# Row-addressed stores from GpSimd in the experts' phase of a two-layer transformer kernel

## The chip, the cores and the metric

The kernel runs on one core of a Trainium2 chip. The metric is the device time of one execution in microseconds (us); before the change its median over 3 runs was 2280.21 us (2277.04 to 2282.47). Engines are named as in the profile: PE (matrix multiply, with PEld for its weight loads), DVE (vector), ACT (activation), POOL (GpSimd) and SP (the engine that here only issues transfers).

## The reference, cut to what matters

The input x has 128 batches of 64 tokens of width 128, that is 8192 rows of 128 float32 numbers. Four blocks follow one another, each added to x:

```
x = x + L0_xattn(layernorm(x), ctx)          # cross attention, 16 heads
x = x + L0_ffn(layernorm(x))                 # 8 experts, each takes its 8 best tokens of a batch
x = x + L1_xattn(layernorm(x), ctx)          # self attention, cross attention, relu block
x = x + L1_ffn(layernorm(x))                 # 16 routed experts (4 per token) + 2 shared ones
return x
```

The last block is the one that the change touches. For each token it computes

```
combine = (one_hot(topk_idx, 16) * tw[..., None]).sum(1)      # 4 experts of 16, weights sum to 2.5
h = einsum('td,edf->etf', x, gate_w);  u = einsum('td,edf->etf', x, up_w)
y = einsum('etf,efd->etd', silu(h) * u, down_w)
out = x + einsum('etd,te->td', y, combine) + (silu(x @ sh_gate) * (x @ sh_up)) @ sh_down
```

The result is stored to HBM as 8192 rows of 512 bytes.

## The kernel before, in words

The program is a chain of phases (setup, attention 0, choice, attention 1, attention 2, relu, experts), each with its own instruction streams for the five engines and a barrier at its end. The phase in question is `experts_phase`. It works in 16 groups of 4 tiles of 128 tokens (`NG` = 16, `TILES` = 4, `TOK` = 512). x stays in SBUF as `x_res`. In a group, `step` runs over 18 experts k (2 shared, 16 routed): PE makes the gate and up products of expert k for all 512 tokens in three partial products each (L1152 to L1154), ACT applies silu (L1102), DVE multiplies (L1313, tile `moe_act`), and PE makes the down product of expert k-2 (L1138; L1147 for the two shared ones). DVE adds it into `acc` (L1325 for the first, L1331 for most others). For four of the experts ACT weighs the product into `part` instead (L1095), and POOL sums these (L1029).

Work of the next group is threaded into the same loop: at k = 0 DVE takes its statistics, POOL makes 1/std with a power (L1044), at k = 2 DVE applies the norm (`norm_apply`, L1201, four tiles, written to `xn`), at k = 3 PE transposes these (`make_xT`, L1117), ACT copies the transposes (L1064, L1065), POOL makes the low part of x from them (`low_rows`, L1006), and in later slots DVE and POOL rank the experts (L1011 and L1013 are POOL's share).

Each engine's stream is in program order; the loops run two groups a turn (`pipelined`). POOL's order within a step is: power for group g+1; `total(g-1)`, which adds `part` to `acc` (L1034) once DVE has finished the last expert of group g-1, at k = 2; `low_rows(g+1)`; then the sums and the ranking. `total` gives `totals`, on which SP waits; SP stores `acc[:, s]` with one transfer of 256 KB (L990). `acc` has two buffers; the first write to one (L1325) waits until the store of two groups earlier has landed (`stored`).

Of the kernel before, what the change touches and what calls it, by code (L numbers as in the profile page):

```python
# [9 lines left out]
I32 = mybir.dt.int32  # L10
# [25 lines left out]
for _n, _w in [("a0", ATTN_W), ("a1", ATTN_W), ("a2", ATTN_W), ("ident", P), ("headmask", 4),  # L36
               ("g1", D), ("b1", D), ("g2", D), ("b2", D), ("g3", D), ("b3", D), ("ff2b", D),
               ("negmask", P), ("kiota", 64), ("resetmask", 256), ("trig", P), ("wr", 32),
               ("ff1", 4 * D), ("ff1b", 4), ("ff2", 4 * D), ("router", 16), ("rbias", 64),
               ("lowmask", 256), ("glowmask", 16), ("ident4", 2 * S)]:  # L40
    COLS[_n] = (_at, _w)
    _at += _w
PACK = _at
# [635 lines left out]
def nth(g, n=1, k=0):  # L679

    return g * n + (k + 1)
# [193 lines left out]
def experts_phase(nc, ps, C, x_res, gate, up, down, w_loaded, out):  # L875

    with ExitStack() as ctx:
# [81 lines left out]
        acc_done = sem("acc_done")  # L959
        part_added = sem("part_added")  # L960
        totals = sem("totals")
        stored = [sem(f"stored{s}_") for s in (0, 1)]

        def one_by_one(t):
# [14 lines left out]

        @block.sync  # L980
        def _(sp):

            for s in (0, 1):
                sp.sem_inc(stored[s], 1)
            with sp.Fori(0, NG // 2) as i:
                for s in (0, 1):
                    g = i * 2 + s

                    sp.wait_ge(totals, nth(g))
                    sp.dma_start(out[bass.ds(g * TOK, TOK), :].rearrange("(t p) d -> p t d", p=P), acc[:, s]  # L990
                                 ).then_inc(stored[s], 16)
            for s in (0, 1):
                sp.wait_ge(stored[s], 16 * (NG // 2) + 1)

        @block.gpsimd
        def _(pool):
            def prep(g, s):
                pool.wait_ge(var_eps, nth(g))
                nc.gpsimd.tensor_tensor(rstd[:, :], veps[:, :], C["mhalf"][:, 0:TILES], ALU.pow).then_inc(rstd_done, 1)
                low_rows(g, s)  # L1000

            def low_rows(g, s):

                pool.wait_ge(x_high, nth(g))
                pool.wait_ge(xT_copied, nth(g))
                nc.gpsimd.tensor_tensor(x_lo[:, s], xnT[:, s], x_hi[:, s], ALU.subtract).then_inc(x_split, 1)  # L1006

            def rank_experts(g):

                pool.wait_ge(routing, before(g, 21))  # L1010
                nc.gpsimd.tensor_tensor(by_tile(eeq), by_tile(eeq), C["lowmask"].unsqueeze(1).broadcast_to((P, TILES, E * E)), ALU.mult).then_inc(routing, 1)  # L1011
                pool.wait_ge(routing, before(g, 22))
                nc.gpsimd.tensor_tensor(by_tile(egt), by_tile(egt), by_tile(eeq), ALU.add).then_inc(routing, 1)  # L1013

            def split_weights():

                for i in range(K // CH):
                    part = slice(i * CH, (i + 1) * CH)
                    pool.wait_ge(w_high, i + 1)
                    nc.gpsimd.tensor_tensor(gate_lo[:, part], gate[:, part], gate_hi[:, part], ALU.subtract)  # L1020
                    nc.gpsimd.tensor_tensor(up_lo[:, part], up[:, part], up_hi[:, part], ALU.subtract
                                            ).then_inc(w_split, 1)

            def add_part(g, j):

                if j > 1:
                    pool.wait_ge(part_added, nth(g, len(OTHERS) - 1, j - 2))
                pool.wait_ge(acc_done, nth(g, K - 1, OTHERS[j] - SH + 1))
                nc.gpsimd.tensor_tensor(part[:, 0], part[:, 0], part[:, j], ALU.add).then_inc(part_added, 1)  # L1029

            def total(g, s):
                pool.wait_ge(part_added, (g + 1) * (len(OTHERS) - 1))
                pool.wait_ge(acc_done, (g + 1) * (K - 1))
                nc.gpsimd.tensor_tensor(acc[:, s], acc[:, s], part[:, 0], ALU.add).then_inc(totals, 1)  # L1034

            def first_prep(g, s):
                prep(g, s)
                split_weights()
                rank_experts(g)

            def step(g, s, first, more):
                if more:
                    pool.wait_ge(var_eps, nth(g + 1))
                    nc.gpsimd.tensor_tensor(rstd[:, :], veps[:, :], C["mhalf"][:, 0:TILES], ALU.pow  # L1044
                                            ).then_inc(rstd_done, 1)
                if not first:
                    total(g - 1, 1 - s)
                if more:
                    low_rows(g + 1, 1 - s)
                add_part(g, 1)  # L1050
                if more:
                    rank_experts(g + 1)
                add_part(g, 2)
                add_part(g, 3)
                if not more:
                    total(g, s)

            pipelined(pool, NG, first_prep, step)

        @block.scalar  # L1060
        def _(act):
# [121 lines left out]
        def _(dve):  # L1183
# [131 lines left out]
            def accumulate(g, s, k):  # L1315

                if k < SH - 1 or k in OTHERS:
                    return
                n = k - SH + 1
                dve.wait_ge(y_ready, nth(g, K - 1, n))  # L1320
                y = YB[k % 2].rearrange("p (t d) -> p t d", d=D)
                if n == 0:

                    dve.wait_ge(stored[s], g * 8 + (1 - 8 * s))
                    V.tensor_tensor(acc[:, s], y, tiles_of(x_res, g), ALU.add).then_inc(acc_done, 1)  # L1325
                    return
                dve.wait_ge(acc_done, nth(g, K - 1, n - 1))
                if n == 1:
                    dve.wait_ge(routing, nth(g, NR, NR - 1))
                for t in range(TILES):  # L1330
                    last = V.scalar_tensor_tensor(acc[:, s, t], y[:, t], comb[:, s, t, k - SH:k - SH + 1], acc[:, s, t],  # L1331
                                                  ALU.mult, ALU.add)
                last.then_inc(acc_done, 1)
# [583 lines left out]
def setup_phase(nc, ps, C, pack_in, q_mask, pack, work):  # L1917

    with ExitStack() as ctx:
# [27 lines left out]
        @block.vector  # L1947
        def _(dve):
            nc.vector.memset(C["mhalf"][:, :], -0.5)
            nc.vector.memset(C["half"][:, :], 0.5)  # L1950
            nc.vector.memset(C["oneb"][:, :], 1.0 / 32)
            nc.vector.memset(work["ones"][:, :], 1.0).then_inc(consts_set, 1)
            dve.wait_ge(pack_loaded, 16)
            for a in range(3):
                bias = COLS[f"a{a}"][0] + 5 * D
                nc.vector.tensor_scalar(C["bkm"][:, a, :], C["headmask"], pack[:, bias + 1:bias + 2], None, ALU.mult
                                        ).then_inc(consts_set, 1)
            bias = COLS["a0"][0] + 5 * D
            nc.vector.tensor_scalar(C["bqs"][:, :], pack[:, bias:bias + 1], SCALE, None, ALU.mult).then_inc(consts_set, 1)
            nc.vector.tensor_copy(C["identb"].rearrange("p f k -> p (f k)"), C["ident4"]).then_inc(consts_set, 1)  # L1960
            dve.wait_ge(qmask_loaded, 64)
            nc.vector.tensor_scalar(C["qmask"], work["qmi"][:, :, :], 0.0, NEG, ALU.is_equal, ALU.mult
                                    ).then_inc(qbias_done, 1)
            dve.wait_ge(qbias_done, 1)
            nc.vector.tensor_reduce(work["any"][:, 0:2], C["qmask"], AX.X, ALU.max).then_inc(qany_done, 1)
            dve.wait_ge(qany_done, 1)
            nc.vector.tensor_scalar(work["any"][:, 2:4], work["any"][:, 0:2], 0.0, SCALE, ALU.is_equal, ALU.mult
                                    ).then_inc(qany_done, 1)
            dve.wait_ge(qany_done, 2)
            for f in (0, 1):  # L1970
                nc.vector.tensor_scalar(work["diag"][:, f, :], C["ident4"][:, S * f:S * f + S],
                                        work["any"][:, 2 + f:3 + f], None, ALU.mult).then_inc(qscale_diag, 1)
            dve.wait_ge(qscale_ready, 1)
            nc.vector.tensor_copy(C["qscale"][:, :], ps[:, 1, 0:64]).then_inc(qscale_copied, 1)


def build(nc, x_in, ctx_in, q_mask, key_mask, pack_in, wqkv_in, woe_in, gate_in, up_in, down_in, out):
    with ExitStack() as ctx:
# [7 lines left out]
        for n, (at, w) in COLS.items():  # L1986
# [6 lines left out]
        C["half"] = sb("half", [P, 8])  # L1993
        C["qmask"] = sb("qmask", [P, 2, S], BF16)[:, :, :]
        C["qscale"] = sb("qscale", [P, S])
        work = {"qmi": sb("qmi", [P, 2, S], I32), "ones": sb("ones", [P, P]), "any": sb("qany", [P, 4]),
                "diag": sb("qdiag", [P, 2, S])}
        setup_phase(nc, ps, C, pack_in, q_mask, pack, work)
# [87 lines left out]
```

## Time and profile before

| | us |
|---|---|
| median of 3 runs | 2280.21 |
| lowest, highest | 2277.04, 2282.47 |
| the profiled execution's own time | 2276.67 |
| its span, first to last instruction | 2274.7 |
| PE busy in the span | 2021.8 (89%) |
| DVE busy | 1738.6 (76%) |
| ACT busy | 1015.3 (45%) |
| POOL busy | 511.8 (23%) |

The experts' phase begins at about 1540 us of the span and lasts to its end. In the row of the profile's page that cuts the span in 40 slices PE shows 8 or 9 tenths in every slice of it but the first, and POOL 2 or 3. Line numbers (L1034) are those of the kernel before. A row of the timeline gives the start, the duration, the engine, the line, what is written and read with its size, and the number of instructions merged in the row; in brackets stands how long the engine was idle before it, and what ended that. "SPq" is the stream of transfers that SP issues.

### The profile page before, as it was taken

To read this page: it belongs to the slowest core of one execution; us is meant where nothing else is said; L and a number is where in the kernel's file an instruction comes from. 1 tells how busy PE (TensorE), PEld (TensorE's weight loads), DVE (VectorE), ACT (ScalarE), POOL (GpSimd) and SP (SyncE) were. 2 spreads that over 40 slices of the span, in tenths; PEclk is the share of its full clock that TensorE was granted. 3 is DMA by queue.
4 is the path that set the end of the run, shared out by engine and by line. 5 is a ranking of instruction groups with operands and counts; after the bars stand their busy time and mean duration, and the time that the engine had idled before them with its cause. 6 is when DMAs were issued, how large, how long until landed. Compare 5 with 4: busy or idle time off the path is not lost. (4 is left out here: it accounts for less than half of the span.)

```text
span 2274.7 us, 52942 instructions
## 1 busy us (share of the span) xinstructions
PE 2021.8 (89%) x19268; PEld 1557.3 (68%) x19268; DVE 1738.6 (76%) x4586; ACT 1015.3 (45%) x1956; POOL 511.8 (23%) x504
## 2 busy tenths in 40 slices
PE   5999995777777999997999997994999999999998
PEld 3666664566664666664677675764888888888887
DVE  4767766677755888887799995665888888888886
ACT  3455452445542444443455553543444444443443
POOL 0101100000001222322122222663222232232221
PEclk9999998899996999998999998996999999999999
DMA  3000000000000000000000001000000000000000
GB/s 121 20 28 28 18 18 1 1 1 0 0 1 1 1 0 0 0 0 19 30 28 28 28 18 63 1 0 0 6 6 10 5 5 10 5 5 9 6 5 10
DMA packets 27248, 30.41 MB, mean 13 GB/s; under 512 B 1936, under 2 KB 20624, under 8 KB 26896
## 3 DMA queue, kind: packets, MB, share of 16 engines
q1 hardware_dynamic: 27152, 29.28, 4.1%
q8 instruction: 42, 0.69, 0.1%
q14 instruction: 54, 0.44, 0.1%
HBM read 25.08 MB, written 4.19 MB: 13 GB/s over the span
## 5 line engine op out<-in xcount | busy, mean ns | idle before, releaser
L320 ACT ACTIVATE ex<-ps 128x512 f32<-128x512 f32 x384 | 228.7, 596 | 335.7 <-PE ps L580 334.5
L1102 ACT ACTIVATE moe_sg<-ps 128x512 f32<-128x512 f32 x288 | 172.6, 599 | 365.0 <-PE ps L1154 364.8
L414 DVE TENSOR_REDUCE mx<-ps 128x8 f32<-128x512 f32 x384 | 262.5, 684 | 62.0 <-PE ps L562 61.2
L580 PEld LDWEIGHTS ps<-pack,sh 128*128 128x128 f32 x1536 | 173.9, 144 | 185.0 <-DVE sh L416 113.3
L580 PE MATMUL ps<-pack,sh 128*128 128x128 f32 x1536 | 253.7, 289 | 44.4 <-DVE sh L416 43.1
L1138 PEld LDWEIGHTS ps<-down,moe_act 128*128 128x128 f32 x2048 | 266.1, 191 | 33.9 <-DVE moe_acc L1331 13.0
L1138 PE MATMUL ps<-down,moe_act 128*128 128x128 f32 x2048 | 271.0, 275 | 7.3 <-DVE moe_acc L1331 7.3
L416 DVE TENSOR_TENSOR sh<-ps,mx 128x512 f32<-128x512 f32 x384 | 265.6, 692 | 13.2
L596 PEld LDWEIGHTS ps<-vblk,ex 128*64 128x64 f32 x6144 | 215.1, 140 | 66.8 <-issue 66.2
L596 PE MATMUL ps<-vblk,ex 128*64 128x32 f32 x6144 | 258.1, 228 | 0.3
L1313 DVE TENSOR_TENSOR moe_act<-ps,moe_sg 128x512 f32<-128x512 f32 x288 | 197.7, 686 | 69.2 <-PE ps L1154 55.2
L1331 DVE SCALAR_TENSOR_TENSOR moe_acc<-ps,moe_comb,moe_acc 128x128 f32<-128x128 f32 x768 | 215.6, 343 | 22.3 <-issue 15.5
L562 PE MATMUL ps<-kblk,qd 32*64 32x256 f32 x3072 | 210.8, 392 | 0.0
L287 ACT ACTIVATE kblk<-ps,bkm,pack 128x512 f32<-128x512 f32 x192 | 143.1, 778 | 69.7 <-PE ps L527 56.8
L1152 PE MATMUL ps<-moe_x_lo,moe_gate_hi 128*128 128x512 f32 x288 | 137.3, 477 | 26.3 <-DVE moe_act L1313 24.8
L562 PEld LDWEIGHTS ps<-kblk,qd 32*64 32x64 f32 x3072 | 108.4, 136 | 52.2 <-issue 6.7
L224 POOL TENSOR_TENSOR rstd<-veps,mhalf 128x4 f32<-128x4 f32 x32 | 32.6, 1017 | 388.4 <-DVE veps L376 388.4
L1029 POOL TENSOR_TENSOR moe_part<-moe_part 128x512 f32<-128x512 f32 x48 | 62.2, 1295 | 253.9 <-ACT moe_part L1095 253.9
L250 POOL TENSOR_TENSOR zg<-z,pack 128x256 f32<-128x256 f32 x64 | 40.8, 638 | 334.3 <-DVE z L459 334.3
L1154 PE MATMUL ps<-moe_x_hi,moe_gate_hi 128*128 128x512 f32 x288 | 114.3, 397 | 0.0
L1152 PE MATMUL ps<-moe_x_lo,moe_up_hi 128*128 128x512 f32 x288 | 114.2, 396 | 0.0
L1153 PE MATMUL ps<-moe_x_hi,moe_gate_lo 128*128 128x512 f32 x288 | 114.0, 396 | 0.0
(232 smaller groups left out, 3663.7 us busy)
## 6 DMA issues: line engine op xcount, KB each, us to landing
ctxT<-in_ctx SPq DMA_DIRECT2D x32, 256.0 KB, 2.8
x_res<-in_x SPq DMA_DIRECT2D x16, 256.0 KB, 2.9
kmi<-in_key_mask SPq DMA_DIRECT2D x16, 256.0 KB, 3.4
out<-moe_acc SPq DMA_DIRECT2D x16, 256.0 KB, 2.3
pack<-in_pack SPq DMA_DIRECT2D x1, 2536.5 KB, 9.2
wqkv<-in_wqkv SPq DMA_DIRECT2D x1, 1536.0 KB, 8.5
gate<-in_gate SPq DMA_DIRECT2D x6, 192.0 KB, 4.0
up<-in_up SPq DMA_DIRECT2D x6, 192.0 KB, 4.1
```

Of the source, the lines that this page charges most:

```text
L287: last = nc.scalar.activation(kblk[:, s, :, j, :], by_batch(PREP), ACT.Identity, bias=bkm[:, j:j + 1], scale=headmask[:, j:j + 1])
L320: nc.scalar.activation(ex[:, u % 2], UB[u % 4].rearrange("p (c n) -> p c n", n=P), ACT.Exp).then_inc(e_ready, 1)
L414: nc.vector.tensor_reduce(mx[:, u % 2], sc, AX.X, ALU.max).then_inc(max_done, 1)
L416: nc.vector.tensor_tensor(sh[:, u % 4].rearrange("p (h k) -> p h k", k=S), sc, mx[:, u % 2].unsqueeze(2).broadcast_to((P, HH, S)), ALU.sub ...
L562: last = nc.tensor.matmul(outs[w][64 * b:64 * b + 64, t * HQ * S:(t + 1) * HQ * S], qd[rows, s, n * S:(n + 1) * S], kblk[rows, s, n].rearr ...
L580: last = nc.tensor.transpose(UB[u % 4][:, c * P:(c + 1) * P], sh[:, u % 4, c * P:(c + 1) * P], ident)
L596: last = nc.tensor.matmul(OB[m][64 * b:64 * b + 64, col:col + 32], ex[:, u % 2, c, b * S:(b + 1) * S], vblk[:, s, 2 * (2 * m + t) + b, pai ...
L1102: nc.scalar.activation(sg[:, k % 2], GB_[k % 2], ACT.Silu).then_inc(silu_done, 1)
L1138: last = nc.tensor.matmul(YB[k % 2][:, t * D:(t + 1) * D], act_[:, k % 3, t * P:(t + 1) * P], down[:, k, :], start=True, stop=True)
L1152: nc.tensor.matmul(out, hi, y, start=True, stop=False)
L1313: V.tensor_tensor(act_[:, k % 3], UB[k % 2], sg[:, k % 2], ALU.mult).then_inc(act_ready, 1)
L1331: last = V.scalar_tensor_tensor(acc[:, s, t], y[:, t], comb[:, s, t, k - SH:k - SH + 1], acc[:, s, t], ALU.mult, ALU.add)
```

## The change

- `out` is no longer written by SP. After each `total`, POOL copies four columns of row numbers into a tile `rowid`, waits for that copy and for its own sum, and then issues four indirect transfers, one for each tile of 128 tokens: partition p of `acc[:, s, t]` goes to the row of `out` whose number stands in `rowid[p, s, t]`. Each counts 16 into `stored[s]`.
- The row numbers are laid into the packed constants on the host (64 more columns, 0 to 8191 column by column) and turned to integers in setup by one more DVE instruction.
- SP's loop now waits for the four transfers of a buffer and gives two counts to a new semaphore `acc_free[s]`, on which DVE's first write of the buffer waits, instead of waiting on `stored[s]` itself. At the end of the phase it is POOL that waits for all transfers.

```
             for s in (0, 1):
-                sp.sem_inc(stored[s], 1)
+                sp.sem_inc(acc_free[s], 1)
             with sp.Fori(0, NG // 2) as i:
                 for s in (0, 1):
-                    g = i * 2 + s
-                    sp.wait_ge(totals, nth(g))
-                    sp.dma_start(out[bass.ds(g * TOK, TOK), :].rearrange("(t p) d -> p t d", p=P), acc[:, s]
-                                 ).then_inc(stored[s], 16)
-            for s in (0, 1):
-                sp.wait_ge(stored[s], 16 * (NG // 2) + 1)
+                    sp.wait_ge(stored[s], (i + 1) * (16 * TILES))
+                    sp.sem_inc(acc_free[s], 2)
...
                 nc.gpsimd.tensor_tensor(acc[:, s], acc[:, s], part[:, 0], ALU.add).then_inc(totals, 1)
+                nc.gpsimd.tensor_copy(rowid[:, s], C["rows"][:, bass.ds(g * TILES, TILES)]).then_inc(rows_set, 1)
+                pool.wait_ge(rows_set, nth(g))
+                pool.sem_inc(passed, 1)
+                pool.wait_ge(totals, nth(g))
+                pool.sem_inc(passed, 1)
+                for t in range(TILES):
+                    nc.gpsimd.indirect_dma_start(
+                        out, bass.IndirectOffsetOnAxis(rowid[:, s, t:t + 1], 0), acc[:, s, t], None
+                    ).then_inc(stored[s], 16)
...
             pipelined(pool, NG, first_prep, step)
+            for s in (0, 1):
+                pool.wait_ge(stored[s], 16 * TILES * (NG // 2))
...
-                    dve.wait_ge(stored[s], g * 8 + (1 - 8 * s))
+                    dve.wait_ge(acc_free[s], g + (1 - s))
                     V.tensor_tensor(acc[:, s], y, tiles_of(x_res, g), ALU.add).then_inc(acc_done, 1)
...
             nc.vector.tensor_scalar(C["bqs"][:, :], pack[:, bias:bias + 1], SCALE, None, ALU.mult).then_inc(consts_set, 1)
+            nc.vector.tensor_copy(C["rows"][:, :], C["rowid"]).then_inc(consts_set, 1)
...
+    put("rowid", np.arange(BATCH * S).reshape(-1, P).T)
```

On POOL, in the experts' loop, this stands around the sum `total` (`moe_acc<-moe_acc,moe_part`) and the low part of x (`moe_x_lo`) before the change:

```order
193 L1032 ISA
194 L1033 REGISTER_ALU
195 L1034 TENSOR_TENSOR moe_acc<-moe_acc,moe_part 128x512
196 L1006 TENSOR_TENSOR moe_x_lo<-moe_xnT,moe_x_hi 128x512
197 L1028 REGISTER_ALU
198 L1029 TENSOR_TENSOR moe_part<-moe_part 128x512
```

and this after it, at the same place (`rows` is the constant table of row numbers, `moe_rowid` the tile that the transfers read):

```order
193 L1030 ISA
194 L1031 REGISTER_ALU
195 L1032 TENSOR_TENSOR moe_acc<-moe_acc,moe_part 128x512
196 L1033 ISA
197 L1033 COPY moe_rowid<-rows 128x4
198 L1039 DMA out<-moe_acc,moe_rowid 8192x128 x4
199 L1004 TENSOR_TENSOR moe_x_lo<-moe_xnT,moe_x_hi 128x512
200 L1026 REGISTER_ALU
```

One small copy and four transfers have moved in between the sum and the low part of x. At the end of POOL's stream, in the last group, the order after the change is:

```order
238 L1027 TENSOR_TENSOR moe_part<-moe_part 128x512 x3
239 L1032 TENSOR_TENSOR moe_acc<-moe_acc,moe_part 128x512
240 L1033 COPY moe_rowid<-rows 128x4
241 L1039 DMA out<-moe_acc,moe_rowid 8192x128 x4
242 L878 UNCONDITIONAL_BRANCH
```

The last sum, which was the last of POOL's instructions in the phase, is now followed by the copy and the four transfers.

## Rows read from the trace of the kernel before

**Rows 1.** Page: busy time of each engine, and the chain that ended last, by engine.

```profile
PE 2021.8 (89%) x19268; PEld 1557.3 (68%) x19268; DVE 1738.6 (76%) x4586; ACT 1015.3 (45%) x1956; POOL 511.8 (23%) x504
...
PE 25%; DVE 4%; issue 2%; ACT 0%; DVEq 0%; POOL 0%; POOLq 0%
```

**Rows 2.** Windows, one group each: length, PE, PEld, DVE, ACT, POOL busy, clock, DMA.

```profile
1707.00:1750.00 43.00, 42.78 (x266) 37.77 (x266) 37.49 (x109) 18.77 (x39) 11.78 (x8) 1.00 0.02 6
1750.00:1795.00 45.00, 43.04 (x267) 37.64 (x266) 37.26 (x109) 18.76 (x39) 11.82 (x8) 1.00 0.02 7
```

**Rows 3.** Waits, 1560 to 2275 us: us in total, times, longest.

```profile
PE ps L1152 <- DVE moe_act L1313: 24.8, 7, 17.1
...
DVE moe_acc L1331 <- issue: 15.5, 13, 2.2
```

**Rows 4.** Timeline around the sum of one group, from 2188.3 us.

```profile
2188.56 1.28 POOL L1034 TENSOR_TENSOR moe_acc<-moe_acc,moe_part 128x512 f32<-128x512 f32 x1 [1.73 <-DVE moe_acc L1331]
...
2189.00 1.71 DVE L1201 TENSOR_SCALAR moe_xn<-x_res,moe_mv,moe_rstd 128x128 f32 x4
2189.12 1.95 PE L1147 MATMUL ps<-down,moe_act 128*128 128x128 f32 x16
...
2190.79 0.47 PEld L1117 LDWEIGHTS ps<-pack,moe_xn 128*128 128x128 f32 x4
...
2191.11 0.69 DVE L1313 TENSOR_TENSOR moe_act<-ps,moe_sg 128x512 f32<-128x512 f32 x1 [0.40 <-PE ps L1147]
...
2192.76 1.28 POOL L1006 TENSOR_TENSOR moe_x_lo<-moe_xnT,moe_x_hi 128x512 fp32r<-128x512 f32 x1 [2.91 <-ACT moe_xnT L1065]
```

**Rows 5.** Lines L1201 and L1331: duration in ns min/median/max, first and last start.

```profile
L1201 DVE TENSOR_SCALAR moe_xn<-x_res,moe_mv,moe_rstd x64: 330/336/936, 1543.5 to 2190.4; 128x128 f32 x56, 128x128 f32<-128x128 f32 x8
...
L1331 DVE SCALAR_TENSOR_TENSOR moe_acc<-ps,moe_comb,moe_acc x768: 335/343/354, 1582.4 to 2269.5; 128x128 f32<-128x128 f32 x192
```

**Rows 6.** Timeline of DVE, cut to the first and the last of that group's four.

```profile
2189.00 0.93 DVE L1201 TENSOR_SCALAR moe_xn<-x_res,moe_mv,moe_rstd 128x128 f32 x1
...
2190.11 0.59 DVE L1201 TENSOR_SCALAR moe_xn<-x_res,moe_mv,moe_rstd 128x128 f32 x2
```

**Rows 7.** A second place where DVE and POOL meet: line L1267, and the timeline.

```profile
L1267 DVE TENSOR_SCALAR moe_gout<-moe_gin x16: 164/170/1271, 1561.4 to 2208.5; 128x16 f32<-128x16 f32 x16
...
1682.69 1.30 POOL L1029 TENSOR_TENSOR moe_part<-moe_part 128x512 f32<-128x512 f32 x1 [14.44 <-ACT moe_part L1095]
1682.75 1.27 DVE L1267 TENSOR_SCALAR moe_gout<-moe_gin 128x16 f32<-128x16 f32 x1
```

**Rows 8.** POOL's instructions by size: duration in ns min/median/max.

```profile
L2080 POOL MEMSET const-float32-0.0<- x1: 98/98/98, 0.2 to 0.2; 128x1 f32 x1
...
L231 POOL COPY xn<-y_res x16: 608/609/610, 1070.2 to 1358.6; 128x512 f32 x14, 128x512 f32<-128x512 f32 x2
...
L224 POOL TENSOR_TENSOR rstd<-veps,mhalf x32: 1007/1017/1025, 20.8 to 1022.6; 128x4 f32<-128x4 f32 x32
...
L1013 POOL TENSOR_TENSOR moe_egt<-moe_egt,moe_eeq x16: 2337/2390/2397, 1566.7 to 2216.5; 128x1024 f32<-128x1024 f32 x16
```

**Rows 9.** Timeline of the end of the span.

```profile
2269.94 1.26 POOL L1034 TENSOR_TENSOR moe_acc<-moe_acc,moe_part 128x512 f32<-128x512 f32 x1 [6.81 <-DVE moe_acc L1331]
2271.37 0.37 SPq L990 DMA_DIRECT2D out<-moe_acc  x1
```

**Rows 10.** The store to `out`: issue time in ns, and us from issue to landing.

```profile
L990 SPq DMA_DIRECT2D out<-moe_acc x16: 372/372/411, 1621.4 to 2271.4; - x16
...
DMA to landing us min/median/max: 2.3/2.3/2.5
```

**Rows 11.** Timeline of setup, once the packed constants have landed.

```profile
9.99 0.49 DVE L1956 TENSOR_SCALAR bkm<-pack 128x4 f32<-128x4 f32 x3 [8.84 <-DMA pack<-in_pack]
...
10.45 0.21 DVE L1960 CAST identb<-pack 128x128 bf16<-128x128 f32 x1
```

**Rows 12.** The next instruction of POOL after L1006 in the same group.

```profile
2208.49 1.30 POOL L1029 TENSOR_TENSOR moe_part<-moe_part 128x512 f32<-128x512 f32 x1 [14.44 <-ACT moe_part L1095]
```

More of the change, by code:

```diff
@@ L39 @@
                ("ff1", 4 * D), ("ff1b", 4), ("ff2", 4 * D), ("router", 16), ("rbias", 64),
-               ("lowmask", 256), ("glowmask", 16), ("ident4", 2 * S)]:
+               ("lowmask", 256), ("glowmask", 16), ("ident4", 2 * S),
+               ("rowid", BATCH * S // P)]:
     COLS[_n] = (_at, _w)
@@ L961, in experts_phase @@
         totals = sem("totals")
+        rows_set = sem("rows_set")
+        acc_free = [sem(f"acc_free{s}_") for s in (0, 1)]
+        rowid = sb("rowid", [P, 2, TILES], I32)
         stored = [sem(f"stored{s}_") for s in (0, 1)]
@@ L1995, in build @@
         C["qscale"] = sb("qscale", [P, S])
+        C["rows"] = sb("rows", [P, NG * TILES], I32)
         work = {"qmi": sb("qmi", [P, 2, S], I32), "ones": sb("ones", [P, P]), "any": sb("qany", [P, 4]),
```

## The prediction

> **What bounds the kernel now.** The page comes first: PE is busy for 89% of the span, DVE for 76%, POOL for 23%, and the chain that ended last is mostly PE [rows 1]. Then the windows of the experts' phase, one group each: PE is busy for 42.8 of 43 us in one group and for 43.0 of 45 us in the next, at full clock [rows 2]. So PE bounds this phase, and the two odd microseconds of every second group are the question of the third view, the waits: PE waited seven times on DVE's product, 17.1 us of it once at the phase's start, so 7.7 us in the other six, and DVE itself stood up to 2.2 us for nothing but "issue", thirteen times, 15.5 us together [rows 3]. That is the turn of the loop. POOL has most of each group free. A store of `out` is on the path only once, in the last group; elsewhere it has a whole group (43 us) before its buffer is written again, against 2.3 us to land [rows 2, 10].
>
> The fourth view, the timeline around the place where the change puts its new work, matters most. POOL's sum runs from 2188.56 to 2189.84. DVE's four norm instructions run from 2189.00 to 2190.71, and PE begins to load the transposes' weights at 2190.79, 0.08 us after them, while its own earlier matmuls end at 2191.07 [rows 4]. PE therefore has next to nothing in hand there: what DVE's norm loses at this place, PE loses.
>
> DVE already loses something to POOL there. The norm instruction takes 336 ns in the median and 936 at most [rows 5]; the long one is the first of the four, 0.93 us, and it ends 0.09 us after POOL's sum does [rows 4, 6]. The same is seen elsewhere: a DVE instruction over 16 columns takes 170 ns in the median and 1271 ns where it stands beside POOL's 1.30 us sum [rows 7]. DVE's accumulations, which take one input from PSUM, are never long, 354 ns at most in 768 [rows 5]; so the norm instructions are the ones at risk.
>
> **The change part by part.**
>
> *End of the kernel.* Before, the last sum ends at 2269.94 + 1.26 = 2271.20, SP issues at 2271.37 and the data lands 2.3 us later, at 2273.7 [rows 9, 10]: 2.5 us after the sum. Now come the copy and its wait, 0.3 us together (a copy between POOL's 98 ns memset of one column and its 609 ns copy of 512 [rows 8], nearer the first, and two short waits), then four issues on POOL one behind the other, T each, and from the end of the last issue to landing what is left of the 2.3 us behind SP's 0.37 us issue, 1.9 us [rows 10]. That is 2.2 + 4T against 2.5, so 4T - 0.3 more. T has no row, since POOL issues no transfer before. Below it is bounded by SP's 0.37 us for all 512 rows [rows 10], above by POOL's longest instruction, 2.39 us over 1024 columns [rows 8]: +1.2 to +9.3 us. I take T = 1.1 us, close to the 1.02 us that POOL needs for a power over four columns [rows 8], because software that treats 128 row numbers should look like POOL's work on few columns with much to do for each. That gives +4.1 us. A transfer could also be quicker than that after its issue; 1.9 us is taken for both kinds.
>
> The Trainium skill ("DMA: Bandwidth & Descriptors", Latency and other measured facts) gives 0.6 us to the first byte for transfers issued by SP and about 1 us for those from GpSimd; by that the sum would be 0.4 us higher, an estimate. No row of before shows a GpSimd transfer.
>
> *The copy of row numbers, in 14 groups.* It starts right behind the sum, at about 2189.9, when three of DVE's four norm instructions are still to run. It is a POOL instruction that reads and writes SBUF, like the sum that held the first of them back. At 0.1 to 0.2 us, held once in each of the 14 groups that norm a next one (56 of the 64 norm instructions lie in these [rows 5]), it costs 0 to 2.8 us; I take 0.1 us each, 1.4 us.
>
> *The issues of the transfers, in the other 15 groups.* POOL works through them from about 2190.2 to 2194.6, then does the low part of x, 1.8 us later than its old start at 2192.76. Its next instruction came at 2208.49, after 14.44 us of idling [rows 4, 12], and PE needs the low part only in the next group. That delay costs nothing. Behind POOL's new wait on its own sum and copy stand only these issues.
>
> *SP's relay and DVE's wait.* DVE now waits for a count that SP passes on after the landing. The last of four landings at about 2196.5 comes some 80 us before that buffer is next written; free. SP has nothing else queued.
>
> *Setup.* One more DVE conversion of 64 columns stands in a chain where 128 columns took 0.21 us, and the constants are 1.3% longer in a load of some 9 us [rows 11]: 0.1 + 0.1 = 0.2 us.
>
> Sum: 4.1 + 1.4 + 0.2 = 5.7 us. On the profiled execution's own 2276.67 us that is 2282.4; this execution lies 3.5 us under the median of the three runs, so against 2280.21 it is 2285.9 us. Slower by 0.25%. What a measurement of this kernel can tell from no change is about 0.2%, 4.6 us.
>
> **The rivals.**
>
> *POOL's issues hold DVE's norm back as its sums do (rival 1).* The first issue starts near 2190.2, and DVE's last norm instruction near 2190.4 (the last two run 2190.11 to 2190.70 [rows 6]). If an issue holds whatever the sum held, for all its T, one norm instruction ends T late, and if DVE and POOL take turns, two of them. The bounds are 0.5 us (half an issue) and 2 x 1.2 us per group, times 14: 7 to 34 us. With one issue of 1.1 us it is 15.4 us on top of 5.7: 2301 us. For it speaks that the sum did exactly this in every group [rows 5]; against it, that building a transfer is not a pass over a tile, and that the last norm instruction may be ahead of it by the 0.2 us in question. It would also do nothing at the end of the kernel, where DVE is idle.
>
> The Trainium skill ("SBUF — State Buffer", Who interferes with whom) says that a GpSimd instruction and certain VectorE ones, tensor_scalar among them, share a port pair, and whichever is first keeps it for the whole instruction. The rows of the sum agree with that (0.93 us instead of 0.34); whether the issue of a transfer counts as such an instruction no row here shows. By that rule this rival is the case.
>
> *The turn of the loop gets cheaper (rival 2, not slower).* DVE's stream in the loop loses two rows that only wait, since its new wait folds into others. If the 2.2 us stand at the turn, which cost PE 7.7 / 6 = 1.3 us each time [rows 3], went away in all seven turns, 9.0 us would come back: 5.7 - 9.0 = -3.3, 2276.9 us. It decides only from 5.7 us, that is where at least four or five turns lose their stall. Nothing in the trace says that a stall at a branch depends on two rows more or less, so it is unlikely.
>
> *A cheap issue (rival 3).* With T near SP's 0.4 us the end costs 1.3 us, the copy hides, and setup adds 0.2: 2281.7 us, which no measurement would tell from before. For it speaks only that SP does it so; POOL has no small instruction over 0.1 us that isn't a power.
>
> **How the numbers follow.** The forecast case 0.48 (its own range 2283 to 2290: T from 0.6 to 1.8 us with the copy at 0 to 0.2 us), rival 1 0.34, rival 3 0.13, rival 2 0.05. The range of 8 in 10 leaves out the cheapest issue and rival 2 below, and the upper quarter of rival 1 above: 2281 to 2304 us. Slower by over 0.2% means above 2284.8: nearly all of rival 1 (0.33) and six tenths of the forecast case (0.30), 0.63. Faster by as much is below 2275.6: 0.04, from rival 2. The rest, 0.33, is within 0.2%.
>
> **What the profile would show.** Right: POOL's issues at the end are back to back, about 1.1 us apart, and the last one is followed by 2 us of nothing; a norm instruction of the first three kinds stays at 0.34 us, and PE's transposes start 0.1 us later behind the sum than before. Rival 1: two long norm instructions in a group instead of one, and PE idle for about 1 us before the transposes in each of 14 groups, so that a pair of groups takes 90 us or more instead of 88. Rival 2: DVE's "issue" waits fall under 10 us. Wrong altogether would be a low part of x that reaches PE late, or a first write of `acc` that waits for SP.

## The result, and the profile after

The changed kernel takes 2287.93 us (median of 18 runs) against 2281.07 us for the kernel before (18 runs, same chip): 1.0033 times as long, 95% interval 1.0022 to 1.0043, that is +5.0 to +9.8 us. It is slower, by 0.3%. The profiled execution took 2285.41 us with a span of 2283.6, which is 8.7 us more than the profiled one of before.

The page of the changed kernel, its busy times and its queues (answers to [rows 1]):

```profile
span 2283.6 us, 53027 instructions
...
PE 2023.7 (89%) x19268; PEld 1558.5 (68%) x19268; DVE 1737.5 (76%) x4587; ACT 1016.4 (45%) x1956; POOL 578.0 (25%) x584
...
q0 software_dynamic: 2048, 4.20, 0.6%
```

POOL is busy for 66 us more, which is the 64 issues and 16 copies, and a queue has appeared that carries the 4.20 MB of the output. PE and DVE do the same work as before.

The same two windows as in [rows 2], one group each (length, then busy time of PE, PEld, DVE, ACT, POOL, then clock and transfers):

```profile
1706.00:1749.00 43.00, 42.48 (x264) 37.58 (x265) 37.44 (x109) 18.46 (x39) 15.94 (x13) 1.00 0.02 6
1749.00:1794.00 45.00, 43.23 (x267) 37.62 (x265) 37.16 (x108) 19.11 (x40) 15.92 (x13) 1.00 0.02 7
```

POOL has 4 us more in each, PE nothing. From the first sum of the phase to the last it is 649.96 us before (1619.98 to 2269.94) and 649.32 after (1619.58 to 2268.90). So the groups cost nothing that can be seen. The timeline of one group shows why (answers to [rows 4]):

```profile
2187.74 1.28 POOL L1032 TENSOR_TENSOR moe_acc<-moe_acc,moe_part 128x512 f32<-128x512 f32 x1 [1.71 <-DVE moe_acc L1340]
...
2188.17 1.70 DVE L1210 TENSOR_SCALAR moe_xn<-x_res,moe_mv,moe_rstd 128x128 f32 x4
...
2188.97 0.18 POOL L1033 COPY moe_rowid<-rows 128x4 int32 x1
...
2190.07 1.08 POOL L1039 DMA_INDIRECT out<-moe_acc,moe_rowid  x1 [0.92 <-POOL moe_rowid L1033]
...
2191.45 0.96 POOL L1039 DMA_INDIRECT out<-moe_acc,moe_rowid  x1 [0.30 <-issue]
```

The copy lies inside DVE's four norm instructions and they still take 1.70 us. The first issue starts at 2190.07, 0.2 us after the last norm instruction (2188.17 + 1.70 = 2189.87), because 0.92 us pass between the copy and it. The two don't meet here. Nor do they elsewhere by the norm's durations: its four instructions keep the times that they had (minimum, median, maximum 330, 335 and 935 ns, against 330, 336 and 936 before [rows 5]; mean of the 56 in the loop 482 against 483).

The loss stands behind the last sum. A term first: a DRAIN is an instruction that stands at the end of the phase on every engine, without a line of its own in the kernel; the trace puts it at the line where the phase's function begins (L878, L877 in the kernel before) and in the engine's queue (POOLq). The end of the timeline, and POOL's own stream there (duration in ns, start):

```profile
2268.90 1.26 POOL L1032 TENSOR_TENSOR moe_acc<-moe_acc,moe_part 128x512 f32<-128x512 f32 x1 [6.79 <-DVE moe_acc L1340]
2270.10 0.19 POOL L1033 COPY moe_rowid<-rows 128x4 int32<-128x4 int32 x1
2271.20 1.00 POOL L1039 DMA_INDIRECT out<-moe_acc,moe_rowid  x1 [0.91 <-POOL moe_rowid L1033]
2272.50 0.97 POOL L1039 DMA_INDIRECT out<-moe_acc,moe_rowid  x1 [0.30 <-issue]
2273.77 0.96 POOL L1039 DMA_INDIRECT out<-moe_acc,moe_rowid  x1 [0.30 <-issue]
2275.04 0.96 POOL L1039 DMA_INDIRECT out<-moe_acc,moe_rowid  x1 [0.30 <-issue]
```

```profile
L878 POOLq COMPARE_BRANCH  x1: 38/38/38, 2277.4 to 2277.4; - x1
L878 POOLq DRAIN  x1: 5289/5289/5289, 2277.5 to 2277.5; - x1
...
L878 SPq EVENT_SEMAPHORE  x1: 17/17/17, 2283.0 to 2283.0; - x1
```

The reader can add it up from the sum's end at 2270.16: 1.04 us to the first issue, 4.80 us for four issues (to 2276.00), 1.4 us until POOL's wait for the landings is over (2277.4), 5.3 us of POOL's DRAIN (from 2277.5 to 2282.8), and 0.8 us to the end at 2283.6. Together 13.4 us. SP's last step of the phase, a semaphore, comes at 2283.0, right behind POOL's DRAIN, though its own DRAIN took 7 ns at 2277.5; the end waits for POOL. The same stretch before, from 2271.20 to 2274.7, was 3.5 us. That is +9.9 us. The span is only 8.9 us longer; the other -1.0 lies ahead of the last sum, 0.4 before the first sum and 0.6 between the sums. Differences of that size aren't explained here: between the first sum and the last the profiled executions of all the kernels here take 648.8 to 651.0 us. The drain was there before too, beside the last sum:

```profile
L877 POOLq DRAIN  x1: 1354/1354/1354, 2269.9 to 2269.9; - x1
```

(this row is of the kernel before; it ended at 2271.26, 0.06 us after the sum).

### The profile page after: what moved, and what is told of

The parts are those of the page before. It is cut to its first block and busy times, and to the rows that moved or that the text cites. A ratio compares the mean times of both kernels' runs of the same rounds, so it can differ in the third digit from the quotient of the medians.

```text
span 2283.6 us, 53027 instructions
## 1 busy us (share of the span) xinstructions
PE 2023.7 (89%) x19268; PEld 1558.5 (68%) x19268; DVE 1737.5 (76%) x4587; ACT 1016.4 (45%) x1956; POOL 578.0 (25%) x584
## 5 line engine op out<-in xcount | busy, mean ns | idle before, releaser
L417 DVE TENSOR_TENSOR sh<-ps,mx 128x512 f32<-128x512 f32 x384 | 265.4, 691 | 13.2
L1322 DVE TENSOR_TENSOR moe_act<-ps,moe_sg 128x512 f32<-128x512 f32 x288 | 197.4, 685 | 60.3 <-PE ps L1163 45.5
L1340 DVE SCALAR_TENSOR_TENSOR moe_acc<-ps,moe_comb,moe_acc 128x128 f32<-128x128 f32 x768 | 215.4, 342 | 31.3 <-PE ps L1147 23.5
L1163 PE MATMUL ps<-moe_x_hi,moe_gate_hi 128*128 128x512 f32 x288 | 114.2, 397 | 0.0
L1163 PE MATMUL ps<-moe_x_hi,moe_up_hi 128*128 128x512 f32 x288 | 113.8, 395 | 0.0
```

The costliest lines, as they stand in the source:

```text
L417: nc.vector.tensor_tensor(sh[:, u % 4].rearrange("p (h k) -> p h k", k=S), sc, mx[:, u % 2].unsqueeze(2).broadcast_to((P, HH, S)), ALU.sub ...
L1163: return nc.tensor.matmul(out, hi, x, start=False, stop=True)
L1322: V.tensor_tensor(act_[:, k % 3], UB[k % 2], sg[:, k % 2], ALU.mult).then_inc(act_ready, 1)
```

## The experiments

Below, "tail" is the time from the end of the last sum to the end of the span: 3.5 us in the kernel before, 13.4 in the changed one. Ratios are to the kernel before on the same chip, with 95% intervals.

**The last group by SP.**

```
-            with sp.Fori(0, NG // 2) as i:
+            with sp.Fori(0, NG // 2 - 1) as i:
...
+            sp.wait_ge(totals, NG)
+            sp.dma_start(out[(NG - 1) * TOK:NG * TOK, :].rearrange("(t p) d -> p t d", p=P), acc[:, 1]
+                         ).then_inc(last_stored, 16)
+            sp.wait_ge(last_stored, 16)
...
+                if isinstance(g, int) and g == NG - 1:
+                    return
                 nc.gpsimd.tensor_copy(rowid[:, s], ...)
```

> The changed kernel, but the last of the 16 groups is stored by SP with one transfer, as before the change; the other 15 go by row-addressed transfers. Theory (the whole loss stands at the end: 1.0 us of copy and start, 4.8 us of four issues, 1.4 us to land, and 5.3 us of POOL's drain): if the drain is a fixed price of having issued transfers on POOL at all, it starts when the last sum ends and outlives SP's store, so the span ends 7 us after the last sum's end (before: 3.5, the changed kernel: 13.4), and the time is about 3 us above the kernel before. If the drain only waits for recently issued transfers, it takes under 1 us and the time is that of the kernel before. Rival (the loss is spread over the groups): the time stays about 7 us above the kernel before.

Measured 2279.07 us, ratio 1.0005 (0.9993 to 1.0017). The tail is 5.9 us (2271.14 to 2277.0), with 15 groups still stored by POOL. The drain of that kernel:

```profile
L878 POOLq DRAIN  x1: 6053/6053/6053, 2270.1 to 2270.1; - x1
```

It begins beside the sum and ends at 2276.15, 5.0 us after the sum, though POOL's last transfer was issued 33 us earlier. So the drain doesn't wait for recent transfers, and SP's store, landed at about 2273.5, has to wait for it. The tail was expected at 7; it is 5.0 + 0.8. The spread-over-the-groups rival falls.

**One group by POOL only.** SP stores 15 groups, POOL the one before the last (the condition `g == NG - 2` around the copy and the four transfers, which count on a semaphore of their own).

> SP stores all groups but the 15th of 16, whose four transfers POOL issues some 38 us before the end. If POOL's drain at the end costs by the number of transfers since the phase began, it is 4/64 of 5.3 us, 0.3 us. If it is fixed once POOL has issued any, 5.3 us. If it waits for recent ones only, under 0.3 us. The row-number copy and the first issue are again 0.9 us apart.

One run, 2276.27 us. The drain took 1557 ns from 2269.6, so it was over at 2271.16, 0.43 us after the sum's end at 2270.73; the tail is 3.8 us. So the drain is not a fixed price of having issued transfers on POOL: four of them leave 0.4 us of it, sixty leave 5.0.

**Plain transfers on POOL.**

```
-                for t in range(TILES):
-                    nc.gpsimd.indirect_dma_start(
-                        out, bass.IndirectOffsetOnAxis(rowid[:, s, t:t + 1], 0), acc[:, s, t], None
-                    ).then_inc(stored[s], 16)
+                nc.gpsimd.dma_start(out[bass.ds(g * TOK, TOK), :].rearrange("(t p) d -> p t d", p=P), acc[:, s]
+                                    ).then_inc(stored[s], 16)
```

> The changed kernel with one plain transfer of 256 KB on POOL for each group in place of the four row-addressed ones, and without the copy of row numbers. If an issue's time goes with the rows in it, one plain issue of 512 rows takes four times 0.96 us, about 3.9 us; if it goes by the transfer, about 1 us, and the last sum's end to the span's end shrinks from 13.4 us to about 9 us (0.9 start, 1 issue, 1.4 landing, 5.3 drain, 0.8). By the latter the time is 4.5 us under the changed kernel. The drain stays at 5.3 us if it belongs to POOL's transfers of either kind, and goes to under 0.3 us if it belongs to the row-addressed ones.

Measured 2279.73 us, ratio 0.9999 (0.9985 to 1.0014). The trace's rows for the transfers and the drain:

```profile
L1035 POOL DMA_DIRECT2D out<-moe_acc x16: 767/813/953, 1623.4 to 2272.0; - x16
...
L878 POOLq DRAIN  x1: 1372/1372/1372, 2275.0 to 2275.0; - x1
```

One issue of 512 rows takes 0.81 us, less than a row-addressed one of 128. The drain takes 1.37 us, neither 5.3 nor 0.3: the expectation asked for the kind of transfer, and the number decides, 16 instead of 64. These 16 transfers carry as many rows and bytes as the 64 did, so the drain doesn't go by those. The tail is 5.8 us (2271.40 to 2277.2) and the time can't be told from the kernel before.

**No wait on POOL for the landings.**

```
             pipelined(pool, NG, first_prep, step)
-            for s in (0, 1):
-                pool.wait_ge(stored[s], 16 * TILES * (NG // 2))
```

> The changed kernel without POOL's own wait for the landings at the end of the phase; SP waits for the same landings already. If POOL's drain is 5.3 us of work of its own, it starts with the last issue's end and the span ends 1.4 us earlier, 12.0 us after the last sum's end. If the drain waits until something that follows the landings is over, it becomes 6.7 us long and the end stays at 13.4 us.

Measured 2285.48 us, ratio 1.0032 (1.0018 to 1.0046).

```profile
L878 POOLq DRAIN  x1: 8933/8933/8933, 2272.9 to 2272.9; - x1
```

The row begins while the issues still run. The tail is 12.0 us (2270.64 to 2282.6), and the drain ended 5.3 us after the last issue did (2276.49 to 2281.8). The first theory holds: the drain is work of POOL's own, and the landing is hidden beside it.

**A drain in every group.**

```
                 add_part(g, 3)
+                nc.gpsimd.drain()
                 if not more:
```

> The changed kernel with a drain of POOL at the end of every group's work, where POOL then idles for several us. So far the drain at the phase's end took 5.29 us after 64 transfers issued by POOL, 5.0 after 60, 1.37 after 16 and about 0.4 after 4: 0.083 us for each. Theory (a drain settles each transfer issued since the drain before it): the drains in the groups take 0.4 us each in idle time, the last one 0.4 instead of 5.3, and the span ends 8.5 us after the last sum's end instead of 13.4; the time lies 2 us above the kernel before (9.9 - 4.9 = 5.0 at the end of the profiled one, so 2 to 5). Rival (the number counts from the program's start, or the work goes by all transfers ever issued): each drain takes longer than the one before it, up to 5.3 us, and the end is unchanged at 13.4.

Measured 2281.96 us, ratio 1.0016 (1.0003 to 1.0030). The drains in the groups and the last one:

```profile
L1062 POOLq DRAIN  x16: 1386/1734/1753, 1610.4 to 2262.2; - x16
```

```profile
L878 POOLq DRAIN  x1: 373/373/373, 2279.0 to 2279.0; - x1
```

A drain in a group starts beside a sum of 1.29 us and ends about 0.44 us after it; the shortest, 1386 ns, is that of the first group, before which nothing was issued. The last one takes 0.37 us for four transfers. The tail is 8.7 us (2271.54 to 2280.2). So a drain settles the transfers issued since the drain before, and once that is done in POOL's idle time, 4.7 of the 9.9 us are gone. The durations lie on one line: 0.37 us for 4 transfers and 5.29 for 64 make 0.082 us for each and 0.045 fixed, which gives 1.36 for 16 (measured 1.37) and 4.96 for 60 (measured 5.0).

**Both together.** The last group by SP and a drain in every group.

> Row-addressed transfers for 15 groups, the last group by SP, and a drain of POOL behind every group's work. If the loss is the end of the kernel alone (issues, landing, and 0.083 us of drain for each transfer since the last drain), nothing of it is left: the last sum's end to the span's end is 3.5 us as in the kernel before (5.9 without the drains, 13.4 in the changed kernel), the groups take the same 649 us from the first sum to the last, and the time is that of the kernel before within its interval. If something else of the 15 groups' transfers costs, it stays above.

Measured 2279.12 us, ratio 1.0003 (0.9990 to 1.0016). The drain ended within 0.1 us of the sum, the tail is 3.4 us (2271.92 to 2275.3), and from the first sum to the last it is 648.8 us. With the end of the kernel mended, 60 row-addressed transfers on POOL leave nothing that these runs can tell (-2.3 to +3.6 us). It isn't measurably faster than the kernel before either, and no experiment points to a version that would be.

**Half the rows in an issue.** In the last group the transfers take partitions 0 to 63 only, so this kernel leaves half of that group's rows out of the result. It was run once.

> In the last group the four transfers carry 64 rows each instead of 128; rows 64 to 127 of its four tiles are not stored. If an issue's 0.96 us goes by its rows, these four take 0.5 us each and the drain falls a little (if it too goes by rows: by 4 x 0.04 us); if it goes by the transfer, they stay at 0.96 us with 0.30 us between them. The other groups stay at 0.96 us.

```profile
2273.28 0.93 POOL L1040 DMA_INDIRECT out<-moe_acc,moe_rowid  x1 [0.91 <-POOL moe_rowid L1033]
2274.51 0.90 POOL L1040 DMA_INDIRECT out<-moe_acc,moe_rowid  x1 [0.30 <-issue]
```

0.90 us for 64 rows and 0.96 for 128: by these two points about 1 ns a row on 0.84 us for the transfer, an estimate. The drain is again 5289 ns for 64 transfers; by rows it would have lost some 0.16 us.

**Row numbers from the constant table.** In the last two groups, without the copy.

```
+                if isinstance(g, int):
+                    pool.wait_ge(totals, nth(g))
...
+                            out, bass.IndirectOffsetOnAxis(C["rows"][:, g * TILES + t:g * TILES + t + 1], 0), acc[:, s, t], None
```

> In the last two groups the transfers read their row numbers straight from the constant table, so the copy into the small tile and its wait are gone there. In the changed kernel the first issue starts 1.04 us after the sum's end: 0.14 us of copy, 0.14 us of waits and 0.76 us in which the trace shows nothing. If the 0.76 us is the way from the copy's write to the issue that reads it, it goes: the first issue starts 0.2 us after the sum. If it is the preparation of a first transfer, as plain transfers on POOL show too (0.61 us after the sum), it stays: 0.6 to 0.9 us after the sum, and the span ends 0.1 to 0.4 us sooner after the last sum than 13.4 us.

```profile
2279.48 1.26 POOL L1032 TENSOR_TENSOR moe_acc<-moe_acc,moe_part 128x512 f32<-128x512 f32 x1 [6.80 <-DVE moe_acc L1348]
2281.55 0.98 POOL L1037 DMA_INDIRECT out<-moe_acc,rows  x1 [0.81 <-POOL moe_acc L1032]
```

The first issue starts 0.81 us after the sum, against 1.04 with the copy, and the tail is 13.2 us. Most of the gap belongs to the first transfer after other work, not to the copy (a plain transfer starts 0.61 us after the sum); what POOL does in it the trace doesn't show. (The one time, 2295.72 us, tells nothing of the edit: this execution was 10 us late already at its first sum, at 1629.96, with the edited code only in the last two groups.)

**The norm moved into the issues.** In two kernels, the changed one and the kernel before, DVE's norm, PE's transposes and ACT's copies come one expert later.

```
-                    if more and k == 2:
+                    if more and k == 3:
                         norm_apply(g + 1, 1 - s)
...
-                    if more and k == 3:
+                    if more and k == 4:
                         make_xT(g + 1, 1 - s)
```

> The changed kernel with DVE's norm of the next group, PE's transposes and ACT's copies of them one expert later (k = 3, 4, 4 instead of 2, 3, 3). The norm instructions then fall at about 0.9 us behind the start of the first issue, into the first three issues. If an issue holds DVE's norm instruction back as POOL's sum does (rival 1 of the prediction), one or more of the four take up to 1 us instead of 0.335 in each of 14 groups, and the group takes 1 to 2 us longer than in the kernel below; if not, all 56 are 0.33 us, the 0.935 us ones go as well, since the sum is over by then, and a group takes the same time as in the kernel below.

> The kernel before with the same shift of the norm, for comparison with the one above: stores by SP, nothing on POOL beside the norm. All norm instructions 0.33 us, a pair of groups 87.7 us or less as in the kernel before, time within 2 us of the kernel before. The difference between this and the one above is then the end alone, 7 to 10 us, if issues do not hold DVE, and 20 to 35 us if they do.

Changed with the shift: 2286.00 us, ratio 1.0039 (1.0026 to 1.0053). Before with the shift: 2278.80 us, ratio 1.0005 (0.9993 to 1.0017). The norm instructions of the first and of the second (ns min/median/max), and in the first a meeting with an issue:

```profile
L1210 DVE TENSOR_SCALAR moe_xn<-x_res,moe_mv,moe_rstd x64: 328/343/564, 1543.5 to 2192.0; 128x128 f32 x56, 128x128 f32<-128x128 f32 x8
...
2190.47 1.08 POOL L1039 DMA_INDIRECT out<-moe_acc,moe_rowid  x1 [0.92 <-POOL moe_rowid L1033]
...
2191.28 1.11 DVE L1210 TENSOR_SCALAR moe_xn<-x_res,moe_mv,moe_rstd 128x128 f32 x4
...
2191.85 0.96 POOL L1039 DMA_INDIRECT out<-moe_acc,moe_rowid  x1 [0.30 <-issue]
```

```profile
L1201 DVE TENSOR_SCALAR moe_xn<-x_res,moe_mv,moe_rstd x64: 336/342/346, 1544.0 to 2193.9; 128x128 f32 x56, 128x128 f32<-128x128 f32 x8
```

The four instructions take 1.11 us across parts of two issues, as long as without any. The worst is 564 ns, 0.22 us over the median, and the mean of the 56 is 354 ns against 342: 0.7 us in the whole kernel. A pair of groups takes 87.4 to 87.7 us in the first and 87.6 to 88.0 in the second, where nothing of POOL stands beside the norm; from the first sum to the last it is 649.4 and 651.0 us. An issue doesn't hold DVE's norm as a sum does.

## Why the prediction was right, and where not

The time and the direction were right: 2285.9 us forecast, 2287.93 measured, inside 2281 to 2304. The place was right in the main: 4.1 of the 5.7 us forecast stood at the end of the kernel, where all of the loss is. Its own sum was +5.7 us; the profiled executions differ by 8.7 and the medians by 6.9. Term by term:

- *End of the kernel*, +4.1 forecast, +9.9 measured. The start was put at 0.3 us and took 1.04. T was put at 1.1 us and an issue takes 0.96, but 0.30 us stand between two, so four take 4.80 instead of 4.4. The landing behind the last issue was put at 1.9 and took 1.4. These three make up +0.6 (0.7 + 0.4 - 0.5). Nearly all of the rest is a term that the sum left out altogether: POOL's drain at the end of the phase, 0.082 us for each of 64 transfers, 5.3 us. Where POOL had issued none, it was over 0.06 us after the sum. The prediction's "the last one is followed by 2 us of nothing" is the step that failed; 7.6 us follow it.
- *The copy in 14 groups*, +1.4 forecast, 0 measured. The copy of 0.18 us overlaps the norm and the norm takes 1.70 us as before. PE begins to load the transposes' weights 2.23 us behind the sum's start in both kernels (2190.79 - 2188.56, and 2189.97 - 2187.74), not 0.1 us later.
- *"What DVE's norm loses at this place, PE loses"* was wrong. The kernel before with the norm moved is rid of the 0.6 us hold in all 14 groups (maximum 346 ns instead of 936 [rows 5], mean 342 instead of 483), 8 us of DVE's time. But its pairs of groups take 87.6 to 88.0 us, no less than the 87.6 to 87.8 of before, and its time doesn't change. That shift moves PE's transposes too, so it isn't a test by itself; the rows of PE are. The first is of the kernel before: the weight loads waited for the norm once, 13.4 us at the phase's start. The second is of the same kernel, the last two of the changed one with the norm moved:

```profile
  PEld ps L1117: 13.4, 1
...
2190.90 0.60 PE L1117 MATMUL ps<-pack,moe_xn 128*128 128x128 f32 x4
...
2191.87 1.05 PE L1147 MATMUL ps<-down,moe_act 128*128 128x128 f32 x8
...
2192.76 0.60 PE L1126 MATMUL ps<-pack,moe_xn 128*128 128x128 f32 x4
```

Before, PE's transposes start 1.78 us after the first of the 16 matmuls ahead of them (2189.12 [rows 4]), 0.111 us for each. With the norm moved and over 0.26 us before the weights are loaded, they start 0.89 us after the first of 8, again 0.111 us for each. So PE stood in its own work and lost nothing before the transposes; that they started right behind the norm was two times close together, not a wait.
- *Issues in the other groups, SP's relay*, 0 forecast and 0 measured (649.3 us between the sums, and 2279.12 us with the end mended). The "80 us" to the next write of the buffer should be about 39: the buffer of the sum at 2188.56 is written again by L1325 at 2235.0. It is ample either way.
- *Setup*, +0.2 forecast. The constants reach DVE at 10.27 us instead of 9.99 [rows 11], and the chain ends at 13.36 + 0.23 instead of 13.12 + 0.23: +0.24 us.
- *Rival 1* didn't happen, for two reasons: the first issue comes 0.2 us after the norm, and where they are made to meet an issue costs at most 0.22 us once in a while. The Trainium skill ("SBUF — State Buffer", Who interferes with whom) lets a GpSimd instruction and a tensor_scalar of VectorE in one of its two-port modes exclude each other for a whole instruction. The sum does that here (0.93 us instead of 0.34 [rows 6]); the mode itself no row shows. The issue of a transfer, 0.96 us long, does not in these runs, so the prediction's step from that rule to the issues doesn't hold.
- *Rival 2*: the waits of DVE put down to "issue" did fall from 15.5 to 5.7 us, which the prediction named as its mark. But those put down to PE's down product rose from 4.9 to 23.5, those put down to the last of the up products (L1154, L1163 after) fell from 55.2 to 45.5, PE's own wait there is 7.8 us beside 7.7, and the pairs of groups take the same time within 0.2 us. The kernel before with only the norm moved shows 4.5 us of "issue" too, without the change. The name of the wait changed, not its cost.
- *Rival 3*: T isn't cheap for row-addressed transfers.

So that the forecast came so near is partly luck. With its terms put right the sum is 5.7 - 1.4 + 0.6 + 5.2 = 10.1 us; the profiled span grew by 8.9 and the median by 6.9. The missing drain was offset in part by a copy that costs nothing, and the upper end of the range, 2304 us, came from rival 1, which didn't happen.

What stays open: what POOL does in the 0.8 us before a first issue and the 0.3 us between issues, and what the drain does with each transfer. Only their lengths were measured. That the medians differ by 6.9 us where the tail alone gives 9.9 lies just outside the interval (+5.0 to +9.8) and wasn't followed further; the lowest of the 18 runs of each differ by 9.0 us (2276.38 and 2285.41).

## What to carry to other kernels

In this kernel transfers on GpSimd that ran beside other work were free, but the phase that ended with them paid about 1 us before the first, 1.27 us for each, the landing, and then a drain that goes by how many were issued since the last drain. Leave the last store to SP, issue few large transfers rather than many small ones, and put a drain into GpSimd's idle time. And a start that follows closely on another engine's end is no proof of a wait: look for the wait itself.

## What the runs showed of the hardware

- A drain of GpSimd took 0.37 us after 4 transfers that it had issued, 1.37 after 16, 5.0 after 60 and 5.29 after 64 (the 16 were plain, the others row-addressed, all on one line). It takes that long even where the last transfer was issued 33 us before, and the count starts afresh after each drain.
- A row-addressed issue took 0.96 us for 128 rows and 0.90 for 64; a plain one of 512 rows 0.81 us; one by SP 0.37 us.
- A sum on GpSimd held VectorE's norm instruction for 0.6 us, the issue of a transfer for 0.22 us at most, a copy of four columns by nothing that shows.
